# Twelve of the 64 gathers of expert results issued between GpSimd's gathers of expert inputs

## The chip, the cores and the metric

The kernel runs on one core of one Trainium2 chip. The metric is the device time of one execution in microseconds (us), as the median of several runs. The shown durations come from one profiled execution of the kernel before.

## What is computed

The program is a two-layer perceiver block on x of shape (16, 64, 256), so T = 1024 tokens of D = 256 numbers: cross attention to a context of 1601 rows, latent attention, a routed feed-forward, a second cross attention, a state-space mixer, and last a mixture of experts. Only the last stage and a little of the mixer matter here. The stage picks K = 8 of E = 64 experts for each token and adds their weighted results:

```python
masked = jnp.where(smask > 0, sc, -jnp.inf)
_, tidx = jax.lax.top_k(masked, K)
tw = jnp.take_along_axis(scores, tidx, axis=1)
tw = tw / (tw.sum(-1, keepdims=True) + 1e-20)
...
w_dense = jnp.zeros((T, E), tw.dtype).at[jnp.arange(T)[:, None], tidx].add(tw)
def body(acc, ws):
    wg, wu, wdn, cw = ws
    hmid = jax.nn.silu(x @ wg) * (x @ wu)
    return (acc + cw[:, None] * (hmid @ wdn), None)
y, _ = jax.lax.scan(body, jnp.zeros_like(x), (We_gate, We_up, We_down, w_dense.T))
```

## The kernel before

The function `experts` (from line 1633) does the last stage in two blocks, a block being a stretch of the program that all engines enter and leave together.

**First block: routing.** SyncE stores the normalised tokens to the DRAM tensor `xn_rows` (L1723). VectorE picks eight experts for each token and gives each of the 8192 (token, choice) pairs a row in a list that is sorted by expert and cut into tiles of 128 rows. An expert with few rows shares a tile: the first part of the list holds one expert to a tile ("whole" tiles), the second three tiles to two experts ("shared"). Tiles are run in rounds of RING = 6. The number of whole rounds and of shared rounds depends on the data; VectorE writes both, less their minima, to `trip` (L1895, L1896), from which every engine loads its loop bounds. For a token the eight rows are sorted: `slots8[..., 0]` is the highest, `slots8[..., 7]` the lowest, and `sloti` is the same as integers. For each rank k VectorE also works out `needed[k]`, the number of rounds after which every token's row of rank k has been stored (L1934 to L1942). TensorE turns the list round into the token of each row (L1775, L1779), and VectorE writes it as `idxt` (L1945 to L1950).

**Second block: the tiles.** For tile n, in ring place m = n % 6, in round g = n // 6:

- VectorE copies the tile's column of `idxt` to `idx` (L2073). It does so in its step for tile n - 5, after it has seen tile n - 6 gathered; so GpSimd is at most some five tiles ahead of TensorE.
- GpSimd waits for that index and gathers the tile's 128 rows of 1 KB from `xn_rows` into `xg` with one indirect DMA (L2171). I call this a **row gather**.
- TensorE turns the rows (L2023), multiplies tile n - 3 with gate and up weights (L2042) and tile n - 6 with down weights (L2060). VectorE copies the turned rows (L2081) and multiplies the hidden values (L2089). ScalarE applies silu (L2141), copies the results (L2146), issues the loads of down weights (L2133) and, one tile later, the store of the results to the DRAM tensor `y_rows` (L2158). SyncE issues the loads of gate and up weights (L2195).

**The results.** GpSimd first issues all row gathers. Then, for rank k = 7 down to 0, `collect(k)` loads `needed[k]` (L2175), waits until that many rounds are stored on all six store semaphores, and issues eight indirect DMAs (L2181), one for each 128 tokens, which bring the rank-k result rows from `y_rows` to `yg`. I call these **result gathers**; there are 64. VectorE works out the eight weights of each token (L2097 to L2114) after its last tile, then adds the weighted results to `xt`, rank 7 first (L2125); ScalarE stores each 128 tokens of `xt` when rank 0 has been added.

What sets the order on GpSimd is that program order alone: a wait in it holds all its later gathers. `run` (from L1982) writes the first twelve tiles of every engine out without a loop and loads `trip` after them.

```python
def collect(k):
    rounds = pool.value_load(needed[0:1, k:k + 1], min_val=1, max_val=MOST + MOST2)
    stored = nc.gpsimd.to_reg(rounds * 16)
    pool.wait_ge(s_rows, 16)
    for m in range(RING):
        pool.wait_ge(s_ys[m], stored)
    for j in range(NT):
        nc.gpsimd.indirect_dma_start(out=yg[:, k, j, :], ...)
run(pool, step, 0)
for k in reversed(range(8)):
    collect(k)
```

**Filling.** A gather may name any of the first 128 tiles of `y_rows`. Tiles 64 to 127 are filled from x by eight DMAs of 1 MB each, issued by SyncE much earlier (L780); ScalarE waits for them before its first store (L2159). The mixer (`state_space`) runs before the experts; there SyncE's last work is to load four quarters of a table (L1256), whose users are ScalarE's exponentials (L1440).

Of the kernel before, what the change touches and what calls it, by code (L numbers as in the profile page):

```python
# [5 lines left out]
F32 = mybir.dt.float32  # L6
I32 = mybir.dt.int32
BF16 = mybir.dt.bfloat16
ALU = mybir.AluOpType
# [3 lines left out]
P = 128  # L13
B, S, D = 16, 64, 256
T = B * S
NT = T // P
# [11 lines left out]
E, FE = 64, 128  # L28
# [12 lines left out]
def perceiver(nc, a, out):  # L41
    with ExitStack() as ctx:
# [13 lines left out]
        neghalf = sb("neghalf", [P, 32])  # L56
        xn_rows = nc.dram_tensor("xn_rows", (T, D), F32).ap()
        ffn_rows = nc.dram_tensor("ffn_rows_dram", (T, D), F32).ap()
        y_rows = nc.dram_tensor("y_rows", ((21 + E // 4) * 6 * P, D), F32).ap()
        s_spare = sem("moe_spare_rows_filled")  # L60
        MOST_TILES = P
        SPARE = -(-(MOST_TILES - T * 8 // P) // NT)
# [50 lines left out]
        class Weights:  # L113
# [8 lines left out]
            def rows(self, name, src):  # L122
                n = a[src].shape[0] // P
                return self.put(name, [P, n, a[src].shape[1]], a[src].rearrange("(h p) e -> p h e", h=n))
# [1033 lines left out]
        def state_space(w, w_moe, sync_first):  # L1158
            st = ExitStack()
            own = lambda name, shape, dt=F32: sb("ss_" + name, shape, dt, own=st)  # L1160
# [77 lines left out]
            with nc.Block(no_gpsimd_drain=True) as block:  # L1238
                @block.sync
                def _(sp):  # L1240
                    sync_first(sp)
                    for g in range(2):
                        sp.wait_ge(s_sc, g + 1)
                        for jj in range(4):
                            sp.dma_start(seg_rows[:, 4 * g + jj, :], segs[32 * jj:32 * jj + NH, g, :]).then_inc(s_st[g], 16)
                    for c in range(2):
                        for h in range(2):
                            if c == 0:
                                sp.wait_ge(s_st[h], 64)
                            for par in range(2):  # L1250
                                sp.dma_start(dec[64 * par:64 * par + 64, c, 4 * h:4 * h + 4, :, :].rearrange("p j l t -> p (j l t)"),
                                             seg_rows[2 * c + par, 4 * h:4 * h + 4, :].rearrange("j x -> (j x)").partition_broadcast(64)
                                             ).then_inc(s_ld[c][h], 16)
                    def load_quarter(c, q):
                        for par in range(2):
                            sp.dma_start(stage[c][q][64 * par:64 * par + 64].rearrange("p j l t -> p (j l t)"),  # L1256
                                         seg_rows[2 * c + par, 2 * q:2 * q + 2, :].rearrange("j x -> (j x)").partition_broadcast(64)
                                         ).then_inc(s_lq[q], 16)
                    load_quarter(2, 2)
                    sp.wait_ge(s_cv, CI)  # L1260
                    load_quarter(2, 0)
                    load_quarter(2, 1)
                    sp.wait_ge(s_pm, 4 * CI)
                    load_quarter(2, 3)
                    for q in range(4):
                        sp.wait_ge(s_lq[q], 32)
                        sp.wait_ge(s_g, 2 * q + 1)
                        if q >= 2:
                            sp.wait_ge(s_e, exps[1] + q + 1)
                        load_quarter(3, q)  # L1270
                @block.tensor
                def _(pe):
                    pe.wait_ge(s_w, n_w)
# [358 lines left out]
        def experts(w):  # L1632
            st = ExitStack()
            own = lambda name, shape, dt=F32: sb("moe_" + name, shape, dt, own=st)
# [24 lines left out]
            latest = own("latest", [P, 8])  # L1659
            latest_row = own("latest_of_choice", [8, 1])  # L1660
            latest_int = own("latest_int", [1, 8], I32)
            needed = own("rounds_needed", [1, 8], I32)
            pick = own("pick", [P, NT, E])
            in_tile = own("in_tile", [P, 2, 4, P, 2], BF16)
            RING = 6
            WRITTEN = 2
            LEAST, MOST = 3, 21
            LEAST2, MOST2 = 2, E // 4
            of_tile = own("of_tile", [P, 2, 4, MOST_TILES, 2], BF16)
            marked = own("marked", [P, 2, 4, MOST_TILES, 2], BF16)  # L1670
            count2 = own("count2", [P, P, 2], BF16)
# [48 lines left out]
            with nc.Block(no_gpsimd_drain=True) as block:  # L1720
# [99 lines left out]
                def _(dve):  # L1820
# [72 lines left out]
                    dve.drain()  # L1893
                    nc.vector.tensor_scalar(by_ring[:], count[:, 0:1], float(LEAST), float(RING * P), ALU.max, ALU.mult)
                    nc.vector.tensor_scalar(trip[:, 0:1], count[0:1, 0:1], float(LEAST), -float(LEAST), ALU.max, ALU.add)  # L1895
                    nc.vector.tensor_scalar(trip[:, 1:2], count[0:1, 1:2], float(LEAST2), -float(LEAST2), ALU.max, ALU.add)  # L1896
                    nc.vector.tensor_scalar(below[:, 0, :], through[:], c_col[:, 0:1], None, ALU.is_le)
                    nc.vector.tensor_scalar(below[:, 1, :], halves[:], c_col[:, 0:1], None, ALU.is_le)
                    dve.drain()
# [39 lines left out]
                    dve.drain()  # L1939
                    nc.vector.tensor_scalar(latest_int[:], latest_int[:], 10, None, ALU.arith_shift_right)  # L1940
                    dve.drain()
                    nc.vector.tensor_scalar(needed[:], latest_int[:], 1, None, ALU.add)  # L1942
                    dve.wait_ge(s_im, NT)
                    token, ones_, twos, fours = (ps[:, 4 + x, 0:MOST_TILES] for x in range(4))
                    nc.vector.tensor_copy(home[:], token)  # L1945
# [29 lines left out]
            def whole_rounds(eng):  # L1975
                return LEAST + eng.value_load(trip[0:1, 0:1], min_val=0, max_val=MOST - LEAST)
            def shared_rounds(eng):
                return LEAST2 + eng.value_load(trip[0:1, 1:2], min_val=0, max_val=MOST2 - LEAST2)
# [37 lines left out]
            with nc.Block(no_gpsimd_drain=True) as block:  # L2016
# [113 lines left out]
                def _(act):  # L2130
# [3 lines left out]
                    def step(n, m, g, q, live):  # L2134
# [20 lines left out]
                        if live(DOWN + 1):  # L2155
                            k, place = n - DOWN - 1, (m - DOWN - 1) % RING
                            act.wait_ge(s_yc, k + 1)
                            act.dma_start(y_rows[ds(k * P, P), :], ysb[:, place, :]).then_inc(s_ys[place], 16)  # L2158
                    act.wait_ge(s_spare, SPARE * 16)  # L2159
                    run(act, step, DOWN + 1)  # L2160
                    for j in range(NT):
                        act.wait_ge(s_ya, j + 1)
# [2 lines left out]
                @block.gpsimd  # L2165
                def _(pool):
                    def step(n, m, g, q, live):
                        ready = nc.gpsimd.to_reg(n + 1)
                        pool.wait_ge(s_rows, 16)
                        pool.wait_ge(s_ic, ready)  # L2170
                        nc.gpsimd.indirect_dma_start(out=xg[:, m, :], out_offset=None, in_=xn_rows,  # L2171
                                                     in_offset=bass.IndirectOffsetOnAxis(ap=idx[:, m:m + 1], axis=0)
                                                     ).then_inc(s_ga[m], 16)
                    def collect(k):
                        rounds = pool.value_load(needed[0:1, k:k + 1], min_val=1, max_val=MOST + MOST2)  # L2175
                        stored = nc.gpsimd.to_reg(rounds * 16)
                        pool.wait_ge(s_rows, 16)
                        for m in range(RING):
                            pool.wait_ge(s_ys[m], stored)
                        for j in range(NT):  # L2180
                            nc.gpsimd.indirect_dma_start(out=yg[:, k, j, :], out_offset=None, in_=y_rows[0:MOST_TILES * P, :],  # L2181
                                                         in_offset=bass.IndirectOffsetOnAxis(ap=sloti[:, 0, j, k:k + 1], axis=0)
                                                         ).then_inc(s_yg[k] if k else s_yl[j], 16)
                    run(pool, step, 0)
                    for k in reversed(range(8)):
                        collect(k)
                    rounds = whole_rounds(pool) + shared_rounds(pool)
                    for m in range(RING):
                        pool.wait_ge(s_ys[m], rounds * 16)
# [181 lines left out]
```

## Time and profile before

| | |
|---|---|
| median of 3 runs | 880.91 us (877.93 to 882.81) |
| the profiled execution | 887.02 us |
| its span, first to last instruction | 885.2 us |
| mean granted TensorE clock | 0.85 of full |
| GpSimd (POOL) busy | 254.1 us, 29% |
| TensorE (PE) busy | 686.7 us, 78% |
| VectorE (DVE) busy | 443.7 us, 50% |
| ScalarE (ACT) busy | 245.3 us, 28% |

The sum of the prediction is made against the profiled execution; its time is 6.1 us above the median of the runs. All times in rows are us from the start of the span. An engine's name with a q (ACTq, POOLq, SPq) is its sequencer, which issues DMAs, loads registers and waits. For a gather on POOL the profile shows the time in which its descriptors are made, not the transfer; the transfer's end is told as "DMA to landing", counted from the issue.

### The profile page before, as it was taken

What the parts mean: (1) busy time and instruction counts of PE and PEld (TensorE: products, weight loads), DVE (VectorE), ACT (ScalarE), POOL (GpSimd) and SP (SyncE); (2) the same over time, 40 slices, a digit from 0 to 9 for tenths busy, and PEclk for the clock granted to TensorE, in tenths of its full rate; (3) what the DMA queues carried; (4) which work ended last, traced back from release to release, by engine and by line L of the source; (5) the groups of instructions that cost most, each with busy time, mean ns of one, the idle gap of its engine ahead of it and who ended that gap; (6) DMA issues with size and microseconds to landing.
All of it is one profiled execution on the core that took longest, in us unless ns stands there. A gap on an engine that the chain in (4) does not pass through costs nothing. (4 is left out here: it accounts for less than half of the span.)

```text
span 885.2 us, 18944 instructions
## 1 busy us (share of the span) xinstructions
PE 686.7 (78%) x6640; PEld 472.5 (53%) x6640; DVE 443.7 (50%) x1121; ACT 245.3 (28%) x471; POOL 254.1 (29%) x289
## 2 busy tenths in 40 slices
PE   5699998977666899899899978797649889994000
PEld 4356565545534456456644467685438778882000
DVE  4333234576673643232346559857943334446923
ACT  1212121564452212121124544203322223331000
POOL 1002000201241120000000445512316445567775
PEclk9899999898776799999889955577788999997555
DMA  9999995580087779998109943001077998996334
GB/s 336 394 412 343 401 411 226 190 286 2 1 309 241 308 306 366 395 391 345 36 7 201 193 111 76 4 2 48 1 193 256 327 307 254 318 319 207 89 101 124
DMA packets 70888, 195.62 MB, mean 221 GB/s; under 512 B 11832, under 2 KB 43552, under 8 KB 65824
## 3 DMA queue, kind: packets, MB, share of 16 engines
q1 hardware_dynamic: 42688, 156.62, 50.4%
q0 software_dynamic: 6816, 18.62, 7.3%
q10 hardware_dynamic: 21312, 19.41, 6.7%
q8 instruction: 46, 0.75, 0.4%
q14 instruction: 26, 0.21, 0.1%
HBM read 181.05 MB, written 21.95 MB: 229 GB/s over the span
## 5 line engine op out<-in xcount | busy, mean ns | idle before, releaser
L2171 POOL DMA_INDIRECT moe_xg<-xn_rows,moe_idx x78 | 74.1, 950 | 81.2 <-DVE moe_idx L2073 71.4
L2181 POOL DMA_INDIRECT moe_yg<-y_rows,moe_sloti x64 | 67.9, 1061 | 19.8 <-issue 18.6
L1475 POOL TENSOR_TENSOR ss_dec<-ss_dec,ss_cT 128x256 f32<-128x256 f32 x48 | 39.7, 862 | 91.5 <-ACT ss_dec L1430 51.0
L2089 DVE TENSOR_TENSOR moe_hidT<-moe_silu,ps 128x128 f32<-128x128 f32 (+1 forms) x64 | 20.3, 317 | 78.4 <-ACT moe_silu L2141 60.1
L1288 PE MATMUL ps<-xnT,w_win 128*128 128x512 f32 x128 | 58.3, 614 | 0.0
L302 PE MATMUL ps<-x0ctxT,x0qcur 128*64 128x512 f32 (+1 forms) x256 | 46.8, 519 | 8.9 <-issue 6.7
L327 PE MATMUL ps<-x1ctxN,x1pT 128*64 128x256 f32 (+1 forms) x416 | 48.2, 390 | 6.7 <-issue 6.1
L1320 PE MATMUL ps<-ss_dec 64*64 64x32 f32 (+2 forms) x1792 | 45.6, 255 | 8.2 <-issue 5.9
L91 POOL TENSOR_TENSOR rstd<-vare,neghalf 128x2 f32<-128x2 f32 (+1 forms) x10 | 11.2, 1124 | 134.3 <-DVE vare L87 134.3
L2141 ACT ACTIVATE moe_silu<-ps 128x128 f32<-128x128 f32 (+1 forms) x64 | 19.3, 302 | 106.7 <-PE ps L2042 58.4
L327 PE MATMUL ps<-x0ctxN,x0pT 128*64 128x256 f32 (+1 forms) x416 | 46.5, 380 | 2.2 <-issue 1.6
L302 PE MATMUL ps<-x1ctxT,x1qcur 128*64 128x512 f32 (+1 forms) x256 | 46.9, 520 | 1.0 <-POOL x1qcur L568 1.0
L1320 PEld LDWEIGHTS ps<-ss_dec 64*64 64x64 f32 (+2 forms) x1792 | 39.6, 172 | 13.9 <-issue 8.0
L327 PEld LDWEIGHTS ps<-x1ctxN,x1pT 128*64 128x64 f32 (+1 forms) x416 | 32.8, 141 | 20.3 <-issue 9.4
L2125 DVE SCALAR_TENSOR_TENSOR xt<-moe_yg,moe_w,xt 128x256 f32<-128x256 f32 x64 | 26.5, 480 | 29.5 <-DMA moe_yg<-y_rows,moe_sloti 29.2
L2042 PE MATMUL ps<-moe_xgT,e_shared_gate_up_weights 128*128 128x192 f32 x224 | 41.2, 327 | 0.0
L1288 PEld LDWEIGHTS ps<-xnT,w_win 128*128 128x128 f32 x128 | 24.9, 198 | 30.2 <-issue 29.8
L2023 PE MATMUL ps<-ident,moe_xg 128*128 128x128 f32 x156 | 32.2, 289 | 10.7 <-DMA moe_xg<-xn_rows,moe_idx 10.6
L1548 DVE COPY_PREDICATED ss_gm<-w_c_lvl,ps 128x128 f32<-128x128 int32 (+1 forms) x80 | 30.8, 384 | 19.1 <-ACT ss_gm L1444 13.6
L2042 PE MATMUL ps<-moe_xgT,moe_gate_up_weights 128*128 128x128 f32 x288 | 39.5, 282 | 0.0
L327 PEld LDWEIGHTS ps<-x0ctxN,x0pT 128*64 128x64 f32 (+1 forms) x416 | 30.6, 137 | 16.3 <-issue 3.8
L302 PEld LDWEIGHTS ps<-x0ctxT,x0qcur 128*64 128x64 f32 x256 | 17.3, 140 | 39.4 <-issue 39.4
(398 smaller groups left out, 1391.0 us busy)
## 6 DMA issues: line engine op xcount, KB each, us to landing
x0ctxT<-ctx_T SPq DMA_DIRECT2D x8, 3202.0 KB, 18.9
x1ctxT<-ctx_T SPq DMA_DIRECT2D x8, 3202.0 KB, 12.8
x0ctxN<-ctx SPq DMA_DIRECT2D x8, 3072.0 KB
x1ctxN<-ctx SPq DMA_DIRECT2D x8, 3072.0 KB
y_rows<-moe_ysb ACTq DMA_DIRECT2D x78, 128.0 KB
moe_gate_up_weights<-moe_gate_up SPq DMA_DIRECT2D x36, 256.0 KB, 4.3
e_shared_gate_up_weights<-moe_gate_up SPq DMA_DIRECT2D x28, 256.0 KB, 4.6
ss_dec<-seg_rows SPq DMA_DIRECT2D x8, 768.0 KB, 17.0
```

The source lines that it names most:

```text
L302: mm = pe.matmul(ps[64 * b:64 * b + 64, n, 0:k1 - k0], qcur[:, u, h, 64 * b:64 * b + 64], ctxT[:, u, b, h, k0:k1], start=h == 0, stop=h == ...
L327: mm = pe.matmul(ps[64 * b:64 * b + 64, 6, 0:D], pT[0:k, u, c, 64 * b:64 * b + 64], ctxN[0:k, u, b, c, :], start=c == 0, stop=c == NC_ - 1)
L1288: mm = pe.matmul(ps[:, 2 * slot[i] + n, :], win[:, h, m * P:(m + 1) * P], xnT[:, h, n * 512:(n + 1) * 512], start=h == 0, stop=h == DH - 1)
L1320: return pe.matmul(dst, f, g, start=True, stop=True)
L1475: e.tensor_tensor(f, f, g, ALU.mult).then_inc(s, 1)
L1548: ins = nc.vector.copy_predicated(old, bc(mask, 1, 4), new)
L2023: mm = pe.transpose(ps[:, TURNED[m % 3], h * P:(h + 1) * P], xg[:, m, h * P:(h + 1) * P], ident[:])
L2042: mm = pe.matmul(ps[:, PRODUCT[place % 3], x * w:(x + 1) * w], weights[:, h, x * FE:(x + 1) * FE], xgT[:, h, col:col + w], start=h == 0, s ...
L2089: nc.vector.tensor_tensor(hidT[:, col:col + w], silu[:, col:col + w], ps[:, PRODUCT[place % 3], w:2 * w], ALU.mult).then_inc(s_hh, tiles)
L2125: ins = nc.vector.scalar_tensor_tensor(xt[:, j, :], yg[:, k, j, :], w8[:, j, k:k + 1], xt[:, j, :], ALU.mult, ALU.add)
L2171: nc.gpsimd.indirect_dma_start(out=xg[:, m, :], out_offset=None, in_=xn_rows, in_offset=bass.IndirectOffsetOnAxis(ap=idx[:, m:m + 1], axis ...
L2181: nc.gpsimd.indirect_dma_start(out=yg[:, k, j, :], out_offset=None, in_=y_rows[0:MOST_TILES * P, :], in_offset=bass.IndirectOffsetOnAxis(a ...
```

## The change

GpSimd issues twelve of the 64 result gathers between row gathers. With `lowest` = `needed[7]`: in round lowest + 2, after the row gathers of places 2 to 5, the gathers of rank 7 for tokens of tiles 0 to 3; in round lowest + 3, at the same places, those of tiles 4 to 7; in the last round, at the same places, four of rank 6. The wait for the stored rounds of a rank stands ahead of its first gather. All other result gathers keep their order behind the rows. For this GpSimd's first twelve tiles are no longer written out, and it loads `trip` (twice) and `needed[7]` before its first row gather.

So that those rounds exist, `trip` now makes the whole number of rounds at least max(needed[7] + 3, needed[6]) + 3; VectorE works this out in a chain of tiny operations ahead of its wait for TensorE. MOST2 and `y_rows` grow by six rounds. SyncE fills tiles 0 to 63 of `y_rows` as well, with eight more 1 MB copies behind its last quarter load in the mixer.

```diff
@@ state_space, SyncE
                         load_quarter(3, q)
+                    for r in range(NT):
+                        sp.dma_start(y_rows[r * NT * P:(r + 1) * NT * P, :], a["x"].rearrange("b s d -> (b s) d")).then_inc(s_spare, 16)
@@ experts
-            LEAST2, MOST2 = 2, E // 4
+            LEAST2, MOST2 = 2, E // 4 + 6
@@ routing, VectorE
-                    nc.vector.tensor_scalar(trip[:, 1:2], count[0:1, 1:2], float(LEAST2), -float(LEAST2), ALU.max, ALU.add)
+                    nc.vector.tensor_scalar(fewest[:, 0:1], count[0:1, 0:1], float(LEAST), None, ALU.max)
@@ routing, VectorE, behind the rounds needed
-                    nc.vector.tensor_scalar(needed[:], latest_int[:], 1, None, ALU.add)
+                    nc.vector.tensor_scalar(needed[:], latest_int[:], 1.0, None, ALU.add)
+                    nc.vector.tensor_scalar(needed_int[:], latest_int[:], 1, None, ALU.add)
+                    dve.drain()
+                    nc.vector.scalar_tensor_tensor(fewest[:, 1:2], needed[:, 7:8], 3.0, needed[:, 6:7], ALU.add, ALU.max)
+                    dve.drain()
+                    nc.vector.tensor_scalar(fewest[:, 1:2], fewest[:, 1:2], 3.0, fewest[:, 0:1], ALU.add, ALU.subtract)
+                    dve.drain()
+                    nc.vector.tensor_tensor(fewest[:, 1:2], fewest[:, 1:2], count[0:1, 1:2], ALU.max)
+                    dve.drain()
+                    nc.vector.tensor_scalar(trip[:, 1:2], fewest[:, 1:2], float(LEAST2), -float(LEAST2), ALU.max, ALU.add)
                     dve.wait_ge(s_im, NT)
@@ ScalarE
-                    act.wait_ge(s_spare, SPARE * 16)
+                    act.wait_ge(s_spare, (SPARE + NT) * 16)
@@ GpSimd
+                    def rows(g, k=None, tiles=()):
+                        for m in range(RING):
+                            step(g * RING + m, m, g, None, None)
+                            if m >= RING - len(tiles):
+                                at = m - RING + len(tiles)
+                                if k is not None and at == 0:
+                                    stored_for(k)
+                                collect(k, tiles[at:at + 1])
-                    run(pool, step, 0)
-                    for k in reversed(range(8)):
-                        collect(k)
+                    total = whole_rounds(pool) + shared_rounds(pool)
+                    lowest = pool.value_load(needed_int[0:1, 7:8], min_val=1, max_val=MOST + MOST2)
+                    with pool.Fori(0, lowest + 2) as g:
+                        rows(g)
+                    rows(lowest + 2, 7, range(0, 4))
+                    rows(lowest + 3, 7, range(4, NT))
+                    with pool.Fori(lowest + 4, total - 1) as g:
+                        rows(g)
+                    rows(total - 1, 6, range(0, 4))
+                    collect(6, range(4, NT))
+                    for k in reversed(range(6)):
+                        stored_for(k)
+                        collect(k, range(NT))
```

`stored_for(k)` is the first half of the old `collect(k)` (load, waits), and the new `collect(k, tiles)` its second half for the named tiles.

## Rows read from the trace of the kernel before

**Rows 1.** Groups by line on POOL from 792 us: busy, mean ns, idle before.
```profile
L2181 POOL DMA_INDIRECT moe_yg<-y_rows,moe_sloti x64 | 67.9, 1061 | 19.8 <-issue 18.6 <-DMA y_rows<-moe_ysb 1.2
```

**Rows 2.** Busy time by stretch of the tile block; last: clock, DMA share, GB/s.
```profile
676.00:734.00 58.00, 52.16 (x360) 44.47 (x358) 21.05 (x84) 15.31 (x56) 26.67 (x29) 1.00 0.96 313
734.00:757.00 23.00, 21.72 (x134) 18.68 (x133) 10.69 (x41) 8.37 (x26) 14.06 (x15) 1.00 0.87 266
757.00:792.00 35.00, 35.00 (x218) 29.18 (x216) 14.42 (x56) 11.04 (x35) 20.81 (x22) 1.00 0.99 327
792.00:808.00 16.00, 13.57 (x76) 10.14 (x74) 6.57 (x22) 5.81 (x18) 11.74 (x14) 1.00 0.90 277
808.00:885.00 77.00, 0.00 (x0) 0.00 (x0) 43.32 (x89) 0.11 (x1) 56.18 (x52) 0.51 0.38 110
```

**Rows 3.** Timeline of POOL: row gathers (L2171) and result gathers (L2181).
```profile
757.36 0.94 POOL L2171 DMA_INDIRECT moe_xg<-xn_rows,moe_idx  x1 [0.51 <-issue]
759.29 0.94 POOL L2171 DMA_INDIRECT moe_xg<-xn_rows,moe_idx  x1 [0.99 <-DVE moe_idx L2073]
760.54 0.94 POOL L2171 DMA_INDIRECT moe_xg<-xn_rows,moe_idx  x1 [0.30 <-issue]
...
791.06 0.95 POOL L2171 DMA_INDIRECT moe_xg<-xn_rows,moe_idx  x1 [0.82 <-DVE moe_idx L2073]
792.61 0.95 POOL L2181 DMA_INDIRECT moe_yg<-y_rows,moe_sloti  x1 [0.60 <-DMA y_rows<-moe_ysb]
...
807.64 1.34 POOL L2181 DMA_INDIRECT moe_yg<-y_rows,moe_sloti  x1 [0.30 <-issue]
...
878.77 0.95 POOL L2181 DMA_INDIRECT moe_yg<-y_rows,moe_sloti  x1 [0.30 <-issue]
```

**Rows 4.** Row gathers of 740 to 800 us: ns min/median/max, and landing.
```profile
L2171 POOL DMA_INDIRECT moe_xg<-xn_rows,moe_idx x33: 942/947/949, 739.5 to 791.1; - x33
...
DMA to landing us min/median/max: 4.5/4.7/5.1
```

**Rows 5.** Timeline of PE: tiles 57 and 77 turned.
```profile
764.98 0.38 PE L2023 MATMUL ps<-ident,moe_xg 128*128 128x128 f32 x2
...
796.97 0.44 PE L2023 MATMUL ps<-ident,moe_xg 128*128 128x128 f32 x2
```

**Rows 6.** The block's start: its barrier, the first row gather, and one register load's parts.
```profile
L1720 POOLq EVENT_SEMAPHORE  x2: 17/17/17, 658.1 to 658.2; - x2
```
```profile
659.43 1.20 POOL L2171 DMA_INDIRECT moe_xg<-xn_rows,moe_idx  x1 [22.70 <-DVE moe_idx L2073]
```
```profile
L2175 POOLq TENSOR_LOAD <-moe_rounds_needed x8: 284/288/434, 791.0 to 852.8; - x8
L2175 POOLq FUSED_REGOPS  x8: 147/148/161, 791.3 to 853.1; - x8
L2175 POOLq SEQ_ASSERT  x8: 18/18/26, 791.5 to 853.3; - x8
```

**Rows 7.** Timeline of VectorE at the end of routing.
```profile
652.23 0.16 DVE L1940 TENSOR_SCALAR moe_latest_int<-moe_latest_int 1x8 int32<-1x8 int32 x1
652.47 0.16 DVE L1942 TENSOR_SCALAR moe_rounds_needed<-moe_latest_int 1x8 int32<-1x8 int32 x1
654.38 0.29 DVE L1945 COPY moe_home<-ps 128x128 f32<-128x128 f32 x1 [1.76 <-PE ps L1779]
```

**Rows 8.** SyncE's last quarter loads and next DMA; ScalarE's use; the present fills' landing.
```profile
543.89 1.09 SPq L1256 DMA_DIRECT2D w_win<-seg_rows  x2
611.02 0.40 SPq L1723 DMA_DIRECT2D xn_rows<-xn  x1
```
```profile
560.93 1.58 ACT L1440 ACTIVATE ss_dec<-w_win,ss_aneg 128x1536 f32<-128x1536 f32 x1
```
```profile
y_rows<-x SPq DMA_DIRECT2D x8, 18.8
```

**Rows 9.** DMA issues of the page: loads of gate and up weights.
```profile
moe_gate_up_weights<-moe_gate_up SPq DMA_DIRECT2D x36, 256.0 KB, 4.3
e_shared_gate_up_weights<-moe_gate_up SPq DMA_DIRECT2D x28, 256.0 KB, 4.6
```

**Rows 10.** The 42nd store of results, and the landing of result gathers of 790 to 806 us.
```profile
753.42 0.34 ACTq L2158 DMA_DIRECT2D y_rows<-moe_ysb  x1
```
```profile
DMA to landing us min/median/max: 3.8/4.1/4.2
```

**Rows 11.** Eight gate and up matmuls at either clock, and busy time by stretch.
```profile
666.88 1.92 PE L2042 MATMUL ps<-moe_xgT,moe_gate_up_weights 128*128 128x128 f32 x8
...
670.57 1.06 PE L2042 MATMUL ps<-moe_xgT,moe_gate_up_weights 128*128 128x128 f32 x8
```
```profile
628.00:632.00 4.00, 1.90 (x9) 1.02 (x7) 3.62 (x17) 1.59 (x6) 1.94 (x4) 1.00 0.00 0
632.00:636.00 4.00, 3.00 (x8) 1.45 (x9) 3.70 (x13) 1.01 (x3) 1.26 (x2) 0.55 0.00 0
...
644.00:648.00 4.00, 2.68 (x42) 2.39 (x42) 2.48 (x5) 2.29 (x3) 0.00 (x0) 1.00 0.86 218
```

More of the change, by code:

```diff
@@ L58, in perceiver @@
         ffn_rows = nc.dram_tensor("ffn_rows_dram", (T, D), F32).ap()
-        y_rows = nc.dram_tensor("y_rows", ((21 + E // 4) * 6 * P, D), F32).ap()
+        y_rows = nc.dram_tensor("y_rows", ((27 + E // 4) * 6 * P, D), F32).ap()
         s_spare = sem("moe_spare_rows_filled")
@@ L1661, in experts @@
             latest_int = own("latest_int", [1, 8], I32)
-            needed = own("rounds_needed", [1, 8], I32)
+            needed = own("rounds_needed", [1, 8])
+            needed_int = own("rounds_needed_int", [1, 8], I32)
+            fewest = own("fewest_rounds", [1, 2])
             pick = own("pick", [P, NT, E])
@@ L2173, in step, with stored_for @@
                                                      ).then_inc(s_ga[m], 16)
-                    def collect(k):
-                        rounds = pool.value_load(needed[0:1, k:k + 1], min_val=1, max_val=MOST + MOST2)
-                        stored = nc.gpsimd.to_reg(rounds * 16)
+                    def stored_for(k):
+                        stored = nc.gpsimd.to_reg(pool.value_load(needed_int[0:1, k:k + 1], min_val=1, max_val=MOST + MOST2) * 16)
                         pool.wait_ge(s_rows, 16)
@@ L2179, in collect @@
                             pool.wait_ge(s_ys[m], stored)
-                        for j in range(NT):
+                    def collect(k, tiles):
+                        for j in tiles:
                             nc.gpsimd.indirect_dma_start(out=yg[:, k, j, :], out_offset=None, in_=y_rows[0:MOST_TILES * P, :],
```

## The prediction

> **What bounds the kernel now.** I read the chain that ended last first, to see which engine the end hangs on; then the groups by line on POOL, the busy time by stretch, and the timelines of POOL, PE and the sequencers where the change cuts in. A result gather occupies GpSimd for 0.95 us when nothing disturbs it, and there is 0.30 us between two; the 64 take 67.9 us busy plus 19.8 idle [rows 1]. From 808 us on TensorE does nothing and GpSimd never stops [rows 2]: the last gather starts at 878.77 [rows 3], and only its landing, one addition and one store follow. So the end is set by when GpSimd has got through its list of DMAs.
>
> While tiles are run, GpSimd is not the bound. From tile 56 on (757.36) to the first result gather (792.61) it issues 22 row gathers in 35.25 us [rows 3]; at 0.95 + 0.30 = 1.25 us each they need 27.5. The rest, **7.75 us, is idle time** waiting for VectorE's indices, while TensorE is busy all the time [rows 2]: a tile costs it (796.97 - 764.98) / 20 = 1.60 us [rows 5].
>
> **Where the moved gathers land.** The order depends on the data. From the choices that the reference makes on its inputs I work out 36 whole tiles and 28 experts in shared ones, which the counts of weight loads confirm [rows 9]: 6 + 7 = 13 rounds, 78 tiles. The rounds needed for ranks 0 to 7 come out as 13, 13, 13, 12, 12, 10, 10, 7. So the new lower bound is max(7 + 3, 10) + 3 = 13: no round is added. Rank 7 is gathered in rounds 9 and 10, behind tiles 56 to 59 and 62 to 65, and four of rank 6 behind tiles 74 to 77. All twelve lie in the 35 us above.
>
> **Term 1, the gathers: GpSimd has one list, so moving work within it gains only idle time that is filled.** Not 12 x 1.25 = 15 us, then, but at most 7.75. Is all of it filled? With a result gather behind it a tile takes GpSimd 2.5 us, more than TensorE's 1.60, so the row gathers fall behind their old times. Tile by tile, each start is the later of (the gather before + 1.25, plus 1.25 for a result gather) and its old time plus TensorE's delay so far: tile 57 starts at 759.86 (0.57 late), 60 is 3.2 late, 66 is 6.1 late; over the undisturbed tiles 66 to 73 it wins some of it back. TensorE has some cover: tile 77 was gathered at 791.06, landed 4.7 us later [rows 3, 4] and was turned at 796.97 [rows 5], 1.2 us to spare; tile 57 had 759.29 + 4.7 against 764.98, 1.0. So TensorE is late by about 6.1 - 1.1 = 5.0 us from tile 66 on. As it has no idle time to catch up with, the indices come 5.0 late as well, and GpSimd, which would be only 3.7 late by tile 74, waits again: 1.3 us of idle time come back. The twelfth result gather then ends its slot at 801.15 instead of 807.64 [rows 3]: **-6.5 us**. With a landing of 3.8 us it would be -7.4, with 5.8 us -5.4. TensorE's own end moves some 6.4 us later and costs nothing: its last results are needed first by rank 2, the 30th gather behind that point, near 840.
>
> The moved gathers themselves take 0.95 us: all 33 row gathers in the rounds took 942 to 949 ns while VectorE worked beside them [rows 4]. The slowing that makes the mean 1061 ns [rows 1] stays with VectorE's weights and additions, which overlap the remaining gathers as before: 0.
>
> **Term 2, the waits for stores.** Rank 7 needs 42 tiles stored. The 42nd store was issued at 753.42 [rows 10]. Its landing is not shown; a weight load takes 4.3 to 4.6 [rows 9], so it is there by 758.0, and GpSimd asks at 758.3, behind tile 56. 0, at most 1.5 if the store lands later; everything behind it in GpSimd's list would wait too. Rank 6 needs 60 tiles and asks behind tile 74; the others ask later than they did relative to their stores, or with 8 us to spare. 0.
>
> **Term 3, the start.** The block's barrier ends at 658.2; the first row gather started at 659.43 [rows 6], which also takes VectorE's first index. Now three register loads come first: 3 x (0.288 + 0.148 + 0.018) = 1.36 us on POOL's sequencer [rows 6], and a loop's setup. The index wait covers some 0.2 of it. I take **+1.3 us**, between 0.2 (if most is covered by the 1.2 us that pass anyway) and 2.5 (if new loop code has to be fetched as well). It carries through: the first tiles, ScalarE's issuing and then TensorE hang on it without slack.
>
> **Term 4, VectorE's chain.** Four links and one more operation, at the 0.24 us from one tiny operation to the next [rows 7], 1.2 us in all; VectorE stood idle for 1.76 us there, waiting for TensorE [rows 7]. 0; if that cover were gone, 1.2.
>
> **Term 5, the eight fills.** Issued by SyncE right behind the last quarter loads, from 545 us [rows 8]. The present eight landed 18.8 us after issue in the median [rows 8], so they are through by some 575; SyncE's next DMA, the store of `xn_rows`, is at 611.02 [rows 8]. The last quarter is used at 560.93, 16 us after its issue [rows 8], and it is ahead of the fills in the same queue. 0; if its landing slipped past that, a few us of the mixer. Without these 36 us of quiet the fills would cost their whole 20 us.
>
> **Sum:** -6.5 + 1.3 = **-5.2 us**: the profiled execution 887.02 goes to 881.8, and the median of the runs, 880.91, to **875.7**, 0.59% less. A measurement of this kernel can tell about 0.5%, 4.4 us, from no change, so the forecast lies just outside of that. The ends of its own range: -7.75 + 0.2 = -7.5 (873.4), and -5.4 + 2.5 = -2.9 (878.0).
>
> **Rival 1: row gathers queue up behind result gathers.** Both are GpSimd's DMAs, and the DMA engines' share is 0.99 in this stretch [rows 2]. If a row gather waits for the result gather ahead of it, it lands up to one spacing (1.25) later, near 5.9: -5.4 + 1.3 = -4.1, 876.8; with the store wait of term 2 as well, -2.6, 878.3. Against it: result gathers issued every 1.25 us under nearly the same load landed in 3.8 to 4.2 us [rows 10], no later than lone row gathers, and the slower rounds move fewer bytes in a us. The Trainium skill, DMA: Bandwidth & Descriptors, Queues, rings and completion order, says that each DMA engine takes the queue rows in turn, a packet at a time, and each row in order. By that rule two gathers in flight would share one turn and this rival would hold; the landings just named do not bear it out.
>
> **Rival 2, the slower side: TensorE loses its high clock.** In rounds 9 and 10 TensorE would work 1.60 of every 2.5 us, 64%, in short pieces. The granted clock was 1.00 all through 676 to 808 us [rows 2], where it was busy 90% and more. In routing it stood at 1.00 with 2.68 of 4 us busy, but fell to 0.55 behind a stretch with 1.90 of 4 [rows 11]. At 1.2 GHz eight matmuls took 1.92 us instead of 1.06 [rows 11], so a tile would take about 1.60 x 1.9 = 3.0 us. GpSimd's pace in the forecast is (798.65 - 757.36) / 21 = 1.97 us, so each tile at the low clock costs 1.1 us of GpSimd's time anew. It decides from 5.2 / 1.1 = 5 tiles, some 14 us, at the low clock; ten tiles give +11 - 5.2 = +5.8, 886.7. The Trainium skill, TensorE: Matmul & The Clock Gate, A second HAM failure mode: psum-queue depth-cycling, tells of short idle pieces between groups of matmuls that made the clock swing. That would speak for this rival; the row with 2.68 of 4 us speaks against it.
>
> **Rival 3: nothing gained.** The idle time comes back in full, because the late row gathers starve TensorE, or a stall at the branches of the new loops (never seen by this trace) takes 3 to 5 us: about 881.
>
> **Rival 4: a round is added.** If on the chip a token's lowest row lay beyond tile 41, or the second lowest beyond tile 59 (I find 39 and 58), six tiles, 9.6 us, would be added: 885.3.
>
> **Chances.** Forecast 0.62, rival 1 0.20, rival 2 0.07, rival 3 0.09, rival 4 0.02. About three quarters of the forecast and a quarter of rival 1 end more than 0.5% lower: faster 0.51. The rest of these two and most of rival 3 are within 0.5%: same 0.40. Slower 0.09. The range of 8 in 10 takes the forecast's low end with the runs' own spread of some 2 us, and on the other side rival 3: 871.5 to 882.0.
>
> **What the profile would show.** Right: 78 row and 64 result gathers; the first result gather near 760, the last row gather near 800; between them POOL with gaps of 0.30 and some 1.3 us more in all; TensorE waiting for gathered rows in rounds 9 and 10, some 5 us in all, and ending near 813; the first row gather near 660.7; y_rows filled by 16 DMAs, none of which delays the mixer. The tail behind it keeps its 1.25 us pace. Wrong: landings of row gathers well over 5 us (rival 1), a clock of 0.5 between 760 and 810 (rival 2), 84 row gathers (rival 4), or a long gap on POOL behind tile 56 (term 2).

## Result, and the profile after

The changed kernel is **slower**: 889.54 us against 881.04, the medians of 20 runs each, ratio 1.0103 (95% interval 1.0084 to 1.0122). That is some +9 us where -5.2 was forecast. Ratios, here and below, are taken over the undisturbed executions alone, so they need not equal the quotient of the medians.

The profiled execution took 889.4 us (its span: 887.6); that of before took 887.0. Those two differ by less than the medians, because the one after had got through the first part of the program, which the change does not touch, 6.4 us sooner (its mean granted TensorE clock up to 537 us was 0.91 of full, that of before 0.90): its last quarter load was issued at 537.54 us, that of before at 543.89 [rows 8]. So I compare stretches between marks inside the traces. The timeline of SyncE's sequencer, after:

```profile
537.54 1.08 SPq L1256 DMA_DIRECT2D w_win<-seg_rows  x2
538.66 5.03 SPq L1272 DMA_DIRECT2D y_rows<-x  x8
619.84 0.39 SPq L1727 DMA_DIRECT2D xn_rows<-xn  x1
```

From the last quarter load to the store of the normalised tokens the mixer needs 619.84 - 537.54 = **82.3 us, where it needed 611.02 - 543.89 = 67.1** [rows 8]. Fifteen us are lost here, in a stage that the change leaves as it was but for these eight copies. The busy time by stretch (columns: us, busy us and number of PE, PEld, DVE, ACT and POOL, clock, DMA share, GB/s), before:

```profile
545.00:570.00 25.00, 21.23 (x783) 18.69 (x777) 22.12 (x44) 8.23 (x10) 18.13 (x19) 0.50 0.14 36
570.00:611.00 41.00, 33.99 (x539) 28.98 (x536) 27.07 (x69) 4.58 (x11) 5.44 (x6) 0.75 0.01 2
```

and after:

```profile
545.00:570.00 25.00, 12.01 (x433) 10.62 (x433) 7.87 (x21) 5.84 (x7) 4.36 (x6) 0.50 0.77 266
570.00:611.00 41.00, 37.36 (x810) 32.04 (x792) 28.23 (x66) 3.72 (x7) 12.08 (x11) 0.68 0.01 3
```

In the first of the two stretches, in which the DMA engines moved 266 GB/s in the mean, TensorE gets 433 matmuls done instead of 783, at the same granted clock of 0.50. VectorE and GpSimd, which work on its results, are busy for less than half of the time they were before (7.87 us of 22.12, 4.36 of 18.13), and ScalarE starts 7 instructions instead of 10. What TensorE waits for is told by its waits in the 30 us from just behind that load (those put down to issue are shown; before had 2.4 us on VectorE besides). Before, then after:

```profile
PE ps L1320 <- issue: 1.4, 3, 0.6
```
```profile
PE ps L1322 <- issue: 12.1, 3, 5.7
PE ps L1354 <- issue: 5.6, 1, 5.6
```

"Issue" is time in which the engine waited for nothing that the profile shows: no data, no semaphore. The timeline of PE after shows them as single holes in a stream of equal matmuls:

```profile
548.10 1.21 PE L1322 MATMUL ps<-ss_dec 64*16 64x16 f32 x33 [5.65 <-issue]
555.93 1.33 PE L1322 MATMUL ps<-ss_dec 64*32 64x32 f32 x50 [4.08 <-issue]
564.87 0.69 PE L1354 MATMUL ps<-ss_gm,ss_xdt 64*64 64x64 f32 x10 [5.55 <-issue]
```

What is missing is the instructions. The DMA queues in a 26 us stretch (columns: packets, MB, share of 16 engines), before from 544 us and after from 538 us:

```profile
q1 hardware_dynamic: 182, 0.82, 12.7%
q8 instruction: 7, 0.11, 1.8%
```
```profile
q1 hardware_dynamic: 402, 9.06, 102.2%
q8 instruction: 3, 0.05, 0.8%
```

Seven loads of instructions before, three after. Each is 16,384 bytes; by the start times of these packets in the trace they follow one another every 3.4 to 5.3 us before, and after 9.0, 7.8 and 8.9 us while the fills run. The fills are 128 packets of 64 KB, eight on each of the 16 DMA engines, 2.9 us each; the last of them has landed 30 us after the first was issued, at 569.

That these loads are TensorE's, and that it waits for them, can be read from their times. After, they start at 545.69, 553.50 and 562.44 us, and the three holes end at 548.10, 555.93 and 564.87: each 2.4 us later. Between two holes TensorE runs 127 matmuls and as many weight loads, which comes to about one load of 256 instructions. Once it has started, a load takes no longer than before (1.1 us, before 0.9 to 1.3); it is its start that comes late.

**The order on GpSimd did what was expected of it.** Its timeline after, to be laid beside [rows 3] and [rows 6]:

```profile
671.06 1.20 POOL L2184 DMA_INDIRECT moe_xg<-xn_rows,moe_idx  x1 [26.36 <-issue]
...
767.36 0.94 POOL L2184 DMA_INDIRECT moe_xg<-xn_rows,moe_idx  x1 [0.50 <-issue]
768.77 0.94 POOL L2194 DMA_INDIRECT moe_yg<-y_rows,moe_sloti  x1 [0.47 <-DVE moe_idx L2086]
770.02 0.95 POOL L2184 DMA_INDIRECT moe_xg<-xn_rows,moe_idx  x1 [0.30 <-issue]
...
796.76 0.95 POOL L2184 DMA_INDIRECT moe_xg<-xn_rows,moe_idx  x1 [0.79 <-DVE moe_idx L2086]
799.92 0.95 POOL L2184 DMA_INDIRECT moe_xg<-xn_rows,moe_idx  x1 [2.21 <-DVE moe_idx L2086]
...
813.22 0.95 POOL L2194 DMA_INDIRECT moe_yg<-y_rows,moe_sloti  x1 [0.30 <-issue]
...
881.28 0.94 POOL L2194 DMA_INDIRECT moe_yg<-y_rows,moe_sloti  x1 [0.30 <-issue]
```

Tile 56 is gathered at 767.36 and the last result gather starts at 881.28: 113.9 us, where it was 878.77 - 757.36 = 121.4 [rows 3]. At the block's start the first index is written at 668.45 and the first row gather starts 2.6 us later (before 1.07).

The stretches of the two profiled executions, in us; each is the difference of two marks in the timelines:

| stretch | before | after | difference |
|---|---|---|---|
| last quarter load to the store of the tokens (mixer) | 67.1 | 82.3 | +15.2 |
| to the first index (routing) | 47.3 | 48.6 | +1.3 |
| to the first row gather (start) | 1.07 | 2.61 | +1.5 |
| to the row gather of tile 56 | 97.9 | 96.3 | -1.6 |
| to the 13th result gather | 50.3 | 45.9 | -4.4 |
| to the last result gather | 71.1 | 68.1 | -3.1 |

The sum is +8.9, the size of the measured change. The differences of routing and of the first 56 tiles are within what the same code shows from run to run (routing 47.3 to 49.1, tiles 0 to 56 96.3 to 98.5 over all profiles). Neither can the -3.1 of the last row be credited to the new order: that stretch takes 67.3 to 68.7 us in all twelve other profiles, four of them in the old order, and the 71.1 of before stands alone. In this pair the order's own gain is the -4.4.

### The profile page after: what moved, and what is told of

Read it like the earlier page. It is cut to its first block and busy times, and to the rows that moved or that the text cites. A ratio compares the mean times of both kernels' runs of the same rounds, so it can differ in the third digit from the quotient of the medians.

```text
span 887.6 us, 18971 instructions
## 1 busy us (share of the span) xinstructions
PE 683.5 (77%) x6640; PEld 473.2 (53%) x6640; DVE 446.0 (50%) x1126; ACT 244.8 (28%) x471; POOL 250.9 (28%) x289
## 5 line engine op out<-in xcount | busy, mean ns | idle before, releaser
L2194 POOL DMA_INDIRECT moe_yg<-y_rows,moe_sloti x64 | 64.8, 1012 | 19.8 <-issue 17.7
L302 PE MATMUL ps<-x0ctxT,x0qcur 128*64 128x512 f32 (+1 forms) x256 | 49.5, 542 | 6.7 <-issue 4.8
L2154 ACT ACTIVATE moe_silu<-ps 128x128 f32<-128x128 f32 (+1 forms) x64 | 19.3, 301 | 113.9 <-PE ps L2055 71.9
L2036 PE MATMUL ps<-ident,moe_xg 128*128 128x128 f32 x156 | 32.6, 293 | 19.0 <-DMA moe_xg<-xn_rows,moe_idx 18.9
L302 PE MATMUL ps<-x1ctxT,x1qcur 128*64 128x512 f32 (+1 forms) x256 | 44.8, 502 | 1.0 <-POOL x1qcur L568 1.0
L2094 DVE COPY moe_xgT<-ps 128x256 f32<-128x256 f32 x78 | 32.7, 421 | 16.4 <-PE ps L2036 15.5
```

The lines of the kernel that those rows point to most:

```text
L302: mm = pe.matmul(ps[64 * b:64 * b + 64, n, 0:k1 - k0], qcur[:, u, h, 64 * b:64 * b + 64], ctxT[:, u, b, h, k0:k1], start=h == 0, stop=h == ...
L2036: mm = pe.transpose(ps[:, TURNED[m % 3], h * P:(h + 1) * P], xg[:, m, h * P:(h + 1) * P], ident[:])
L2094: nc.vector.tensor_copy(xgT[:, :, m * P:(m + 1) * P], ps[:, TURNED[m % 3], 0:D].rearrange("p (h t) -> p h t", h=DH)).then_inc(s_xc, 1)
```

## Experiments

Two theories stood at first. **A:** the fills hold up the loads of TensorE's instructions. **B:** they are harmless and the new order loses the time. The profile spoke for A, but the part had to be run alone, and there was a second question: is it the amount of traffic (**C**) or the size of its packets?

### The fills alone, and the order alone

```diff
# e1: the kernel before
                         load_quarter(3, q)
+                    for r in range(NT):
+                        sp.dma_start(y_rows[r * NT * P:(r + 1) * NT * P, :], a["x"].rearrange("b s d -> (b s) d")).then_inc(s_spare, 16)
...
-                    act.wait_ge(s_spare, SPARE * 16)
+                    act.wait_ge(s_spare, (SPARE + NT) * 16)
```

> The kernel before plus the eight fills alone, at the place of the change. Theory A (the fills hold up the loads of TensorE's instructions in the mixer, each load standing behind 64 KB packets): +13 to +16 us against the kernel before, idle time of TensorE put down to issue of 10 us or more between the last quarter load and the end of the mixer, and no change behind the mixer. Theory B (the fills are harmless and the loss comes from the new order on GpSimd): within 2 us of the kernel before.

Measured: 896.85 us against 882.16 (four runs), ratio 1.0156 (1.0087 to 1.0225), mixer 82.6 us; behind it 120.9 us from tile 56 to the last gather, as in the old order. TensorE's waits from 543 to 573 us:

```profile
PE ps L1322 <- issue: 12.3, 3, 4.9
PE ps L1354 <- issue: 5.6, 1, 5.6
```

Theory A, and B is out: the fills alone give the whole loss.

```diff
# e2: the changed kernel
-                    for r in range(NT):
-                        sp.dma_start(y_rows[r * NT * P:(r + 1) * NT * P, :], ...).then_inc(s_spare, 16)
...
-                            nc.gpsimd.indirect_dma_start(out=yg[:, k, j, :], out_offset=None, in_=y_rows[0:MOST_TILES * P, :],
+                            nc.gpsimd.indirect_dma_start(out=yg[:, k, j, :], out_offset=None, in_=y_rows[0:(42 if k == 7 else 60 if k == 6 else MOST_TILES) * P, :],
```

> The change without its eight fills; so that no unwritten row can be named, the gathers of rank 7 name only the first 42 tiles and those of rank 6 the first 60, which is right for these inputs. Theory A: the loss of the mixer is gone, and what is left is the gain of the new order: 5 to 8 us less than the kernel before (the trace of the changed kernel shows about -4.4 in the tile rounds, -3.1 in the tail, +1.5 at the block's start). Theory B: no faster than the kernel before.

Measured: 879.66 us against 882.16, ratio 0.9968 (0.9929 to 1.0008): less than expected, and not clear of no change. The trace has the marks as forecast, 114.5 us from tile 56 to the last gather and a mixer of 69.0; the latter and routing (48.5) were on the long side in this execution. The timed gain of 0.3% stayed behind the 5 to 8 us expected, and more versions below measure it again. Even without fills TensorE's issue waits in the 30 us behind the last quarter load came to 5.6 us here and 5.2 in e4 below, where before had 1.4; these two have the longest mixers without fills, and the gap between instruction loads that spans the quarter load is 6.3 and 6.1 us in them. It looks as if 0.8 MB of quarter load can hold such a load up as well; no run tests that.

### Where and how the fills do harm

```diff
# e3: the changed kernel, every fill cut in two over half rows
+                        rows_of = y_rows[r * NT * P:(r + 1) * NT * P, :].rearrange("r (h d) -> h r d", h=2)
+                        x_of = a["x"].rearrange("b s (h d) -> h (b s) d", h=2)
+                        for h in range(2):
+                            sp.dma_start(rows_of[h], x_of[h]).then_inc(s_spare, 16)
...
+                    act.wait_ge(s_spare, (SPARE + 2 * NT) * 16)
```

> The change with each 1 MB fill cut into two DMAs over 512 bytes of each row, so the same bytes at the same place in packets of 512 bytes instead of 64 KB. Theory A with the packet size as its cause: TensorE's instruction loads get their turn, most of the 15 us come back, 875 to 879 us by the median of the kernel before at 881. Theory C (the instruction loads suffer from the amount of traffic, whatever its packets): as the change, or worse, since small packets keep the DMA engines busy longer.

Measured: 884.48 us against 882.16, ratio 1.0037 (0.9995 to 1.0080), mixer 75.1 us. About half of the loss came back, not most of it. Issue waits of TensorE from 539 to 569 us:

```profile
PE ps L1325 <- issue: 9.2, 5, 3.2
PE ps L1357 <- issue: 1.6, 1, 1.6
```

The holes are shorter (3.2 us at most, not 5.7), and there are more of them. The expectation was too simple: the size of packets matters, and so does the traffic itself. The fills took 32.6 us in all, little more than the 30.3 of the large packets. Two doses on the kernel before:

```diff
# g3: four fills instead of eight
+                    for r in range(NT // 2):
...
# g4: eight fills, each in two DMAs over alternate groups of four rows (4 KB)
+                        rows_of = y_rows[r * NT * P:(r + 1) * NT * P, :].rearrange("(q t r) d -> t q (r d)", t=2, r=4)
+                        x_of = a["x"].rearrange("b s d -> (b s) d").rearrange("(q t r) d -> t q (r d)", t=2, r=4)
...
```

> The kernel before with four of the eight fills at the place of the change: half the traffic time. Theory A: two to three instruction loads of TensorE are held up instead of four to five, the mixer grows by 6 to 9 us instead of 15. A fixed cost of the fills (an order, a wait, a slow first access) would give 15 as with eight.

Measured: mixer 76.7 us (one round: 891.82 us, ratio 1.0139). Half the fills cost about 10 us of 15, a little more than expected and clearly less than with eight: a dose, not a fixed cost.

> The kernel before with the eight fills in packets of 4 KB instead of 64 KB (alternate groups of four rows, two DMAs to a fill). Theory A with the packet size as the cause: an instruction load waits for short packets only, the mixer grows by 2 to 6 us instead of 15. Theory C (the amount of traffic, or TensorE's load sharing HBM with it): 12 to 15 us as with 64 KB.

Measured: mixer 76.0 us (one round: 891.89 us, ratio 1.0140). Between the two expectations. The waits of TensorE in these two runs from 538 to 580 us, g3 and then g4:

```profile
PE ps L1322 <- issue: 12.4, 6, 5.1
PE ps L1354 <- issue: 0.3, 1, 0.3
```
```profile
PE ps L1325 <- issue: 9.0, 4, 3.5
PE ps L1357 <- issue: 4.3, 1, 4.3
```

| fills at this place | mixer, us | longest gap between instruction loads while they run, us |
|---|---|---|
| none (eight profiles) | 66.3 to 69.4 | 5.2 to 6.3 |
| 8 MB in 512 byte packets | 75.1 | 6.8 |
| 8 MB in 4 KB packets | 76.0 | 7.3 |
| 4 MB in 64 KB packets | 76.7 | 8.4 |
| 8 MB in 64 KB packets (two runs) | 82.3, 82.6 | 9.0, 8.7 |

With small packets some 8 us of the loss are left; packets of 64 KB add another 7. Each row is one execution, or two, and without fills the mixer varies by 3 us, so the order of the three middle rows is not shown. How a load of instructions waits inside a DMA engine these runs don't show either.

```diff
# e4: the changed kernel, its fills moved behind the store of the tokens
...
                     sp.dma_start(xn_rows.rearrange("(j p) d -> p j d", p=P), xn[:]).then_inc(s_rows, 16)
+                    for r in range(NT):
+                        sp.dma_start(y_rows[r * NT * P:(r + 1) * NT * P, :], ...).then_inc(s_spare, 16)
```

> The change with its eight fills issued behind the store of the normalised tokens, at the start of routing. Theory A: the mixer runs as before; routing has shorter programs, but its engines need instruction loads too, so a loss of 0 to 8 us there; in all 873 to 883 us. If the traffic hurt only through the mixer's straight-line matmul program, 874.

Measured: 880.20 us against 882.16, ratio 0.9971 (0.9929 to 1.0012); mixer 69.4, routing 47.8 us. The same 8 MB in the same packets cost nothing measurable beside routing: e2, without fills, had 0.9968. In the mixer TensorE runs 783 matmuls and 777 weight loads in 25 us, 1560 instructions or six loads of 256; in the 29 us of routing from 611 us it ran 111 and 112. In e4 no load of TensorE's instructions started between 586.9 and 631.6 us, while the fills ran from 613 on: there was only this one that they could hold up.

### The versions that keep the gain

```diff
# g1: e4, and GpSimd's first two rounds written out ahead of its register loads
+                    for g in range(2):
+                        rows(g)
                     total = whole_rounds(pool) + shared_rounds(pool)
...
-                    with pool.Fori(0, lowest + 2) as g:
+                    with pool.Fori(2, lowest + 2) as g:
```

> The change with its fills issued behind the store of the normalised tokens, and with GpSimd's first two rounds written out again ahead of its register loads. Against the same without the second edit (880.2): the start of the tile block goes from 2.6 us back to 1.07, and the time falls by that 1.5 us if the start carries through (my term 3), or not at all if something behind it hides it. In all 5 to 7 us less than the kernel before by the trace's terms (-7.2 on GpSimd), where the timed run without this edit gave only 0.3% less.

Measured: 877.28 us against 881.63, ratio 0.9970 (0.9939 to 1.0000), which is 2.6 us and less than the 5 to 7 expected; start 1.06 us. The three loads cost the 1.5 us of the start in every trace that had them there, and none without. The medians of e4 and g1 are 2.9 us apart, but they were run on different chips and the ratios are alike, so the timed runs don't show that it carries through.

> The same new order and written-out rounds, but all sixteen fills at the old place, at the start of latent attention. Theory A (TensorE's instruction loads suffer under 64 KB packets wherever TensorE runs through a long straight program): some of the 15 us may show up there instead; if that stage has few instructions in those 20 us, 0 to 3 us lost, and the whole is 3 to 6 us below the kernel before. Compare with the version whose fills lie in routing.

This has all sixteen fills at the old place (L780) instead. Measured: 875.70 us, ratio 0.9950 (0.9918 to 0.9983); mixer 66.4. Its control has those fills and the old order:

> The kernel before plus the eight fills alone, at the old fills' place in latent attention; GpSimd's order is the old one. If traffic only hurts beside a long straight program on TensorE: 0 to +2 us against the kernel before, mixer 66 to 69 us. Against the version with the new order and the same fills (g2) it is the control: from there the order alone should bring -6 us (from tile 56 to the last gather about 120 us in the old order, 114 in the new).

Measured: 881.78 us against 882.56, ratio 0.9982 (0.9958 to 1.0007); mixer 66.3, 118.8 us from tile 56 to the last gather. The early fills cost nothing that can be told. They do slow TensorE's instruction loads there, which start 9.5 to 13 us apart from 188 us on, where before has 8 to 10; but in the 59 us from 166 TensorE runs only some 600 matmuls and as many weight loads, about 20 instructions a us instead of 60, and none of its waits from 170 to 235 us is put down to issue. The order on GpSimd is what differs between h1 and g2: 118.8 - 112.8 = 6.0 us by the marks. The timed runs show less: 0.9982 against 0.9950 is 2.8 us, and the intervals overlap. (The medians differ by 6.1, but g2 and h1 were run on different chips.) h2 and h3 below were timed beside h1.

```diff
# h3: g2 with rank 7 alone
-                    rows(total - 1, 6, range(0, 4))
-                    collect(6, range(4, NT))
-                    for k in reversed(range(6)):
+                    rows(total - 1)
+                    for k in reversed(range(7)):
```

> As g2, but only the eight of rank 7 are moved, the four of rank 6 stay behind the rows. If a moved gather gains only filled idle time: the four of the last round fill the idle time of places 3 to 5, about 1 to 1.5 us, so this version is that much slower than g2. If each moved gather gained its own 1.25 us, 5 us slower.

Measured: 878.35 us, ratio 0.9949 (0.9919 to 0.9979); 114.0 us from tile 56 to the last gather, 1.3 more than g2. The ratio does not tell it from g2, and 114.0 lies within the 112.8 to 114.5 of the six profiles with twelve moved gathers. The mark before it tells more, as it varies less: from tile 56 to the 13th result gather h3 takes 46.8 us, those six 45.2 to 46.0, the five profiles of the old order 50.3 to 52.5. So eight moved gathers gain about 4 us and twelve about 5, not 10 and 15: only filled idle time is gained.

```diff
# h2: g2 with rank 7 spaced out
-                    rows(lowest + 2, 7, range(0, 4))
-                    rows(lowest + 3, 7, range(4, NT))
-                    with pool.Fori(lowest + 4, total - 1) as g:
-                        rows(g)
+                    spaced(lowest + 2, (3, 5), 7, range(0, 2), True)
+                    spaced(lowest + 3, (1, 3, 5), 7, range(2, 5), False)
+                    spaced(lowest + 4, (1, 3, 5), 7, range(5, 8), False)
```

`spaced` issues a round's row gathers with one result gather behind each named place; its rounds are written out for the 13 rounds of these inputs.

> As g2, but rank 7's eight result gathers stand behind every second row gather of three rounds instead of behind four in a row of two; rank 6's four as before (written for the 13 rounds of these inputs). If TensorE's lateness is what gives idle time back, it is smaller in rounds 9 to 11, at most 1.5 us of idle come back instead of 3, and the time is 1 to 2 us below g2. If the idle time is all that counts and it is filled either way, the same as g2.

Measured: 874.70 us against 882.56, ratio **0.9911 (0.9877 to 0.9946)**: faster than both kernels, and clear of h1 (0.9958 at the least), which has the same fills and the old order. Timeline of POOL:

```profile
756.35 0.94 POOL L2184 DMA_INDIRECT moe_xg<-xn_rows,moe_idx  x1 [0.48 <-issue]
758.24 0.94 POOL L2184 DMA_INDIRECT moe_xg<-xn_rows,moe_idx  x1 [0.95 <-DVE moe_idx L2086]
759.66 0.94 POOL L2194 DMA_INDIRECT moe_yg<-y_rows,moe_sloti  x1 [0.47 <-DMA y_rows<-moe_ysb]
760.90 0.94 POOL L2184 DMA_INDIRECT moe_xg<-xn_rows,moe_idx  x1 [0.30 <-issue]
...
867.58 0.95 POOL L2194 DMA_INDIRECT moe_yg<-y_rows,moe_sloti  x1 [0.30 <-issue]
```

From tile 56 to the last gather it takes 867.58 - 756.35 = 111.2 us, and only 0.8 us of idle time beyond the 0.30 gaps is left up to the 13th result gather; in g2 that was 2.7, in the other five profiles of the changed kernel's order 3.2 to 3.5, in the old order 7.6 to 9.6. That is as the first of the two expectations has it. The 13th result gather comes 43.3 us behind tile 56, 1.9 us less than in g2; the timed runs don't tell h2 from g2, as their intervals overlap.

## Why the prediction was wrong

**Term 5 failed.** It asked whether the fills would delay a transfer that the kernel itself issues: the last quarter load ahead of them, and the store of `xn_rows` behind them. Both answers were right: the quarter load landed in time (the longest of its kind took 5.8 us), and the fills were through 30 us after the first was issued, as the 575 of the forecast has it. But "0" needed a third question, who else uses the DMA engines at that time. The page's own list of queues has two of kind instruction, and TensorE's 1792 small matmuls in a straight line live on one of them. The price is some 15 us: 82.3 and 82.6 against 66.3 to 69.4 without fills. The trace of before held the warning: the DMA share of 0.14 for 545 to 570 us was read as room, and TensorE's few holes "issue" at that place were not asked about. The page of before has them in its line of these matmuls:

```profile
L1320 PE MATMUL ps<-ss_dec 64*64 64x32 f32 (+2 forms) x1792 | 45.6, 255 | 8.2 <-issue 5.9
```

The Trainium skill, Runtime: NRT & Kernel Launch, Instruction fetch mechanics, says that an engine's instructions come in blocks of 16 KiB, 256 instructions, over a DMA queue of the sequencer's own, and calls crossing a block mostly hidden. The block size agrees with the trace (16,384 bytes a load); in the mixer it is hidden only while nothing else fills the DMA engines, and there not wholly: 1.4 us in the 30 us above.

None of the rivals had this mechanism, so the result lies outside of all of them and of the range. The expected sign "none of which delays the mixer" is the one that failed. The rest of the sum and the rivals:

- **Term 1 was right in its mechanism and 1 to 2 us too large.** -6.5 was forecast for the twelfth gather's slot, that is for the 13th result gather. There the pair of profiles shows -4.4, and five profiles of the old order (mean 50.9) against six of the new one (45.8) show -5.1. Up to the last gather the same profiles have 118.8 to 121.4 us (mean 119.9) and 112.8 to 114.5 (mean 113.9), -6.0; that this is nearer to -6.5 is in part luck, as the slow tail of before counts in it. What was mis-sized is the idle time that comes back: 3.3 us in the changed kernel instead of 1.3. Two things that were priced as rivals showed. The landing of row gathers from 760 to 792 us went up from 4.5 / 4.7 / 5.1 us [rows 4] to

```profile
DMA to landing us min/median/max: 4.2/5.5/6.2
```

  That is thin: the trace tells the landing of one row gather in six, here tiles 54, 60 and 66. Tiles 60 and 66, each behind a group of moved gathers, landed in 5.5 and 6.2 us, and in 5.1 to 6.0 in the three other traces of the new order that tell them (e2, e3, g1), against 4.1 to 4.7 in two of the old one (g3, h1); tiles 57 and 63 in e4, behind the first gather of a group, took 4.9 and 4.0. So rival 1 came in part, behind the groups. And the clock was low for 3.4 us near 783, between the two groups (rival 2, far short of its 14 us):

```profile
770.00:780.00 10.00, 8.12 (x50) 6.27 (x48) 3.77 (x15) 3.12 (x10) 7.56 (x8) 1.00 0.97 322
780.00:790.00 10.00, 9.96 (x52) 8.88 (x53) 3.40 (x12) 2.29 (x7) 7.57 (x8) 0.83 0.92 295
```

  The clock is not what gave the idle time back: in e3 it fell only behind the 13th result gather, and the same 3.3 us came back. TensorE's waits for gathered rows in the tile rounds were 6.6 us, near the 5 expected:

```profile
PE ps L2036 <- DMA moe_xg<-xn_rows,moe_idx: 6.6, 6, 1.9
```

- **Terms 2 and 4 were right**: the first result gather came 1.41 us behind tile 56's, 0.16 more than without a wait, and VectorE still had 0.74 us to spare behind its longer chain.

```profile
663.62 0.29 DVE L1958 COPY moe_home<-ps 128x128 f32<-128x128 f32 x1 [0.74 <-PE ps L1783]
```

- **Term 3 was right**: +1.3 forecast, +1.5 in the trace. Neither of its bounds was met; no trace shows new loop code to cost anything more.
- **Rivals 3 and 4** did not come: the gain of the order is there in six traces, the first 56 tiles took 96.3 to 98.5 us under the new loops and 97.9 to 98.3 under the old ones, and there are 78 row gathers.

With the price of term 5 the sum would have been -6.5 + 1.3 + 15.2 = +10.0, and with the measured -5.1, 1.5 and 15.2 it is +11.6, against a measured 9 or so. The rest lies within the 3 us by which the mixer varies without fills and is not accounted for.

## What to carry to other kernels

A quiet DMA share is not free room: look at which engine runs long straight code there, and count its instruction loads, before filling it with bulk copies; put those beside a stage in which TensorE issues few instructions. Smaller packets took back only half of the loss here. On an engine that works through one list, moving work forward gains the idle time that it fills and no more, and in the one version that tried it, it filled more when spaced out than in groups that make the next engine late. When a change needs something on the side (here eight copies so that every row has been written), price that as carefully as the change itself: here it cost two and a half times what the new order brought.

## What was not expected of the hardware

- Bulk copies from DRAM to DRAM (358 GB/s in all from 545 to 570 us of e1) stretched the interval between TensorE's 16 KB instruction loads from some 3.6 us to 7.8 to 9.0 us with 64 KB packets, to 6.5 to 7.3 with 4 KB and, with 512 bytes, mostly to 5.4 to 6.8. The same copies beside routing or latent attention cost nothing that the runs could tell.
- GpSimd's indirect DMAs took 0.95 us each in both places; 64 result gathers had a mean of 1061 ns before [rows 1] and 1000 to 1025 ns in the twelve other profiles, so part of that row was chance of how they met VectorE's work.
